# The second 16-bit part of queries and keys subtracted on GpSimd instead of VectorE

## The reference, cut to what matters

```
q, k, v = (heads(wq, bq), heads(wk, bk), heads(wv, bv))
q = _apply_rope(q, cos, sin)
k = _apply_rope(k, cos, sin)
att = jnp.einsum('bhtd,bhsd->bhts', q, k) * scale
...                                   # causal mask, softmax, times v
x = _layernorm(x + attention)
x = _layernorm(x + experts)           # gate, up, silu, down; weighted sum of 8 rows
```

## Time and profile before

| | |
|---|---|
| median of 3 runs | 2205.56 us (2202.02 to 2207.1) |
| profiled execution | 2201.4 us, span of its instructions 2199.6 us |
| mean granted TensorE clock | 0.935 of full speed |
| PE, DVE, ACT, POOL busy | 1818.1, 1600.4, 1357.2, 1245.4 us |
| L1653, the subtraction, on DVE | 32 instructions |
| L884, the row scatters, on POOL | 512 instructions, 530.4 us busy |

### The profile page before, as it was taken

The page is one execution under the profiler, slowest core; times in us unless marked ns, Lnnn a source line. Parts: engine busy times, 40 slices in busy tenths (PEclk is TensorE's granted clock), DMA queues, the critical chain, the costliest instruction groups (busy, mean ns, idle before and its releaser), DMA issues. The chain is left out here.

```text
span 2199.6 us, 53918 instructions
## 1 busy us (share of the span) xinstructions
PE 1818.1 (83%) x17104; PEld 1298.8 (59%) x17104; DVE 1600.4 (73%) x3572; ACT 1357.2 (62%) x3265; POOL 1245.4 (57%) x1206
## 2 busy tenths in 40 slices
PE   4899888988898889888987997989888888989930
PEld 2455554554555445454544886878777777878720
DVE  3788777877889788777873554565447778869988
ACT  1566655665655455554544876788776777888830
POOL 1003455446444654556544777777777777777760
PEclk8999999999999999999988999999999999999975
DMA  5466677667756875667666865656688899989977
GB/s 165 135 186 195 210 249 232 191 218 245 235 189 219 288 239 191 209 230 240 199 197 240 282 198 189 214 172 207 213 289 294 295 305 313 301 274 354 368 240 252
DMA packets 290570, 520.19 MB, mean 236 GB/s; under 512 B 46328, under 2 KB 192191, under 8 KB 280528
## 3 DMA queue, kind: packets, MB, share of 16 engines
q1 hardware_dynamic: 206400, 324.46, 47.1%
q0 software_dynamic: 58368, 163.70, 20.1%
q10 hardware_dynamic: 25536, 28.58, 3.9%
HBM read 284.54 MB, written 259.20 MB: 247 GB/s over the span
## 5 line engine op out<-in xcount | busy, mean ns | idle before, releaser
L1297 ACT ACTIVATE pT<-ps 128x512 f32<-128x512 f32 (+2 forms) x1008 | 676.6, 703 | 394.4 <-PE ps L1073 312.2
L884 POOL DMA_INDIRECT x_sorted<-xhl,idx x512 | 530.4, 1036 | 500.5 <-DVE xhl L1735 229.0
L1660 DVE TENSOR_REDUCE mn<-ps 128x1 f32<-128x512 f32 (+3 forms) x704 | 412.6, 632 | 57.5 <-PE ps L1047 55.1
L1139 PE MATMUL ps<-pT,gu_hi 128*128 128x256 f16 (+1 forms) x1600 | 372.1, 251 | 42.3 <-ACT pT L1297 42.1
L1140 PE MATMUL ps<-pT,gu_hi 128*128 128x256 f16 (+1 forms) x1600 | 371.1, 250 | 0.0
L1141 PE MATMUL ps<-pT,gu_lo 128*128 128x256 f16 (+1 forms) x1600 | 371.0, 250 | 0.0
L902 POOL DMA_INDIRECT y_tokens<-work,yidx x264 | 279.2, 1058 | 79.8 <-issue 61.8
L1045 PE MATMUL ps<-stacks 96*128 96x512 bf16 (+3 forms) x1024 | 274.7, 311 | 45.0 <-DVE mn L1660 24.0
L1071 PE MATMUL ps<-stacks 99*128 99x512 bf16 (+3 forms) x1024 | 285.7, 310 | 16.2 <-ACT pT L1297 12.6
L1073 PE MATMUL ps<-maskk,identb 128*128 128x128 bf16 x1024 | 223.0, 223 | 0.0
L1205 PE MATMUL ps<-dn,vx 128*128 x608 | 168.0, 276 | 49.3 <-DVE cosT L1868 14.6
(11 more groups left out here) (255 smaller groups left out, 3866.7 us busy)
## 6 DMA issues: line engine op xcount, KB each, us to landing
stacks<-y_tokens SPq DMA_DIRECT2D x64, 1024.0 KB
stacks<-qk_parts SPq DMA_DIRECT2D x128, 384.0 KB
qk_parts<-pbuf SPq DMA_DIRECT2D x62, 384.0 KB
attention<-yev ACTq DMA_DIRECT2D x64, 256.0 KB
qk_parts<-pbuf SPq DMA_DIRECT2D x62, 256.0 KB
stacks<-x_sorted SPq DMA_DIRECT2D x52, 304.0 KB, 4.4
x_sorted<-pads_h SPq DMA_DIRECT2D x99, 152.0 KB
pbuf<-x_sorted SPq DMA_DIRECT2D x40, 304.0 KB
```

The costliest lines, as they stand in the source:

```text
L884: pool.indirect_dma_start(xsort[g][:, :], bass.IndirectOffsetOnAxis(ap=at, axis=0), xhl_rows[:, t, :], None).then_inc(s_scat, 16)
L1139: mmul(o, w_hi[k], x_hi[k], start=k == 0, stop=False)
L1297: return nc.scalar.activation(o, i, f, **k)
L1660: V.tensor_reduce(mn[:, tt, h0:h0 + nh], ps[:, odd_bank("max", at, m), 0:nh * n].rearrange("p (a n) -> p a n", a=nh), axis=AX.X, op=ALU.ma ...
```

## The change

The subtraction of the parts leaves DVE's list inside the loop and enters POOL's, in front of the scatters of steps 5 and 11. Operands, waits and the semaphore that it raises stay the same. Batch 0's two subtractions ahead of the loop stay on DVE, so 30 of the 32 move.

```diff
@@ POOL @@
+            def last_part(b, n):
+
+                at = 2 * b + n
+                wait(pool, s_rest, at + 1)
+                wait(pool, s_part, part_count(b, n, 1))
+                nc.gpsimd.tensor_tensor(parts(b, n)[:, :, 2, :], rotated(b, n)[:, :, :], parts(b, n)[:, :, 1, :],
+                                ALU.subtract).then_inc(s_pp, 1)
...
             for i in range(NB):
                 for e in range(STEPS):
+                    if i < NB - 1:
+                        for n in range(2):
+                            if e == SLOT_LAST[n]:
+                                last_part(i + 1, n)
                     routing(i, e)
@@ DVE @@
                             if e == SLOT_REST[n]:
                                 rest(i + 1, n)
-                            if e == SLOT_LAST[n]:
-                                last_part(i + 1, n)
```

## The result

The changed kernel takes 2223.93 us (median of 7 runs, 2217.94 to 2231.88), the kernel before beside it 2207.1 us (7 runs, 2202.02 to 2216.66). The ratio is 1.0082 (95% interval 1.0057 to 1.0107): 0.8% slower, 17 us by the medians. The profiled execution took 22.4 us longer in span, 2222.0 against 2199.6 us.

What follows compares the result with a forecast made beforehand. It took a train of transfers in a full queue, releasing DVE and PE, as the bound: 14 x 1.28 = 17.9 us on 2201.4 gives 2219.3, or 2223.5 over the median; forecast 2221, 8-in-10 range 2206 to 2238.

Steps and rivals of the forecast that it cites:

- What bounds the turn: In each batch's pass, queued transfers from the queries' parts to the reciprocals' landing hold DVE's multiplication and PE; 21.1 us.
- The rival by which the shift is absorbed: Landing depends on the reciprocals' issue, not the first transfer's start; about 2205 us, no change; chance 0.15.
- POOL's duration: Each moved subtraction takes 2.5 us on POOL, range 0.90 to 2.95, so the queries' one ends 1.28 us late.
- The scatters behind it: POOL's later scatters fall behind, but their end costs nothing; about one more among the queued transfers, 0.4 us, left to range.
- The sign that I had named for this: From the queries' subtraction's end to DVE's multiplication should stay near 21 us in turn 4.
- The sum: Turns 1 to 14 lose 1.28 us each, 17.9 us; turn 0 and the expert stage nothing.
- POOL as the bound: Subtraction takes 2.95 us and late scatters add 0.4 us in 13 turns; 2231 us; chance 0.17.
- The rotation: DVE's `rotate` starts 0.40 us late, beside the transfers' 1.28; DVE idles 0.5 to 1.5 us before `rope` of the keys.
- The keys: POOL's keys' subtraction delays SP's issue of their parts by 1 us, covered because SP has nothing behind them until 384.93.
- The wait for the landing: DVE's wait for `xTden` grows from 48.6 us by more than 1.28 a turn, since DVE also arrives earlier.
- The clock: PE's clock falls to 0.50 as PE resumes; a longer stand-still may keep it low longer, a possible error.
- VectorE as the bound: Freeing DVE of subtractions ahead of row maxima pays if POOL takes under 1.22 us; about 2192 us; chance 0.08.

Runs made afterwards that it cites:

- The late train alone: Kernel before with one more wait on SyncE, so the queries' parts are issued later, after VectorE's first rope step of the keys; 2216.1 us, 1.0063.
- queries only: Changed kernel with the keys' subtraction back on VectorE, only the queries' one on GpSimd; 2233.1 us, 1.0131 to the kernel before.
- keys only: Changed kernel with the queries' subtraction back on VectorE, only the keys' one on GpSimd; 2201.55 us, 0.9985 to the kernel before.
- subtracted twice: Kernel before with the queries' subtraction in the loop done twice on VectorE, the second raising the semaphore; 2217.11 us, 1.0067.
- scatters late only: Kernel before with GpSimd doing an unread stand-in subtraction at the same two places, real subtractions staying on VectorE; 2214.23 us, 1.005.
- the same, root early: Kernel before with GpSimd's unread stand-in subtractions and its reciprocal root moved from behind step 19's scatters to behind step 17's; 2198.23 us, 0.9976.
- train and scatters late, root early: Kernel before with SyncE's extra wait before the queries' parts, GpSimd's unread stand-in subtractions and the earlier reciprocal root; 2221.61 us, 1.0086.

## Why the prediction was right, step by step

The time was forecast at 2221 us and came out at 2223.93; the place and the way of the loss were right, and two sizes were off in opposite senses.

*What bounds the turn.* Right. The late train alone gives 1.0063, and in the changed kernel the landing moved while the reciprocals' issue kept its place. The rival by which the shift is absorbed falls in turns 2 to 14. Turn 1, which has no scatters, stays open: there the landing, from ACT's copy, was 18.05 us before and 17.80 after, but 19.08 with the train late alone. Two readings of the DMA engines were too wide. They were not lightly used all the way up to 358: the share 0.31 is of the last 3 us, and from 349 to 352 it was 0.81. Nor is the queue full throughout: from the issue of the parts to the multiplication the share is 0.93 on the mean over turns 2 to 14, and 0.90 in the changed kernel.

*POOL's duration.* The mis-sized term. I took 2.5 us as the middle of two ways to stack memset passes; it is 2.13. The subtraction is 0.90 us longer, not 1.28, and the sum by this term is 14 x 0.90 = 12.6 us in place of 17.9. The figure of the Trainium skill ("GPSIMD Engine Reference", "Performance versus the Vector engine") would have come nearer: half of its 4497 ns, as an estimate, is 2.25 us, and the trace agrees to 0.12.

*The scatters behind it.* I let their end cost nothing and left their part in the train to the range. Their end did cost nothing in the changed kernel, where the wait for the root is 3.7 us as before. But the landing moved by 1.49 us a turn, 0.59 more than POOL's extra 0.90, and that is the term I left out: over 13 turns 7.7 us. The sign that I had named for this, about 21 us from the end of the queries' subtraction to the multiplication in turn 4, hid it: it reads 21.25 there, but over turns 2 to 14 the mean went from 19.67 to 20.21.

The count of scatters seems to contradict this: 11.3 in the train before, 11.0 in the changed kernel. What it hides is the first us behind the issue. The parts' own packets start only 0.8 us after their issue. In the kernel before 0.85 of a scatter starts in that first us, and the DMA engines' share in it is 0.50. In the five kernels of the table that hold the scatters at the queries' place none does, and the share is 0.10 to 0.12. So 0.4 us of the engines stand empty, and I take that scatter to ride in the train instead. By the last column, the landing should move by the train's delay and 0.41 us for each scatter more than 10.46:

| kernel | worked out, us | measured, us |
|---|---|---|
| the change | 0.95 + 0.22 = 1.17 | 1.49 |
| queries only | 1.93 | 2.27 |
| keys only | -0.62 | -0.46 |
| train late only | 1.11 | 1.14 |
| subtracted twice | 0.71 | 0.73 |
| scatters late only | -0.22 | -0.08 |
| the same, root early | -0.24 | -0.16 |
| train and scatters late, root early | 1.27 | 1.40 |

So the scatters let go inside the train (0.22 us) and POOL's start 0.05 us later behind the copy make about half of the 0.59 that the sum lacked. What is left, at most 0.34 us, is hardly above the 0.3 on which I don't build, and it stays open. The count ends at the landing and so depends on it; it is an account of these runs and no test of its own.

*The sum.* As turn 1 did not move, 13 x 0.90 = 11.7 us and 7.7 make 19.4, beside 20.4 measured in the attention stage and 17 in the medians. The agreement of 17.9 with these is in part luck: a subtraction taken 0.38 us too long stood in for a train taken 0.59 us too short.

*POOL as the bound.* That rival had the term which the sum lacked, 0.4 us in 13 turns for late scatters in the train. Its long subtraction did not come, and the reciprocal root was not late.

*The rotation.* I had it 0.40 us late, beside the train. The numerators' issue came 0.07 us later after the subtraction's start (mean 8.28 against 8.21 us). DVE waited 25.2 us for POOL in 14 turns, 1.8 us each, above my 0.5 to 1.5: the reduction in front of it was done even sooner than I took.

*The keys.* In turn 4 their parts go out 17.94 us after the queries' subtraction starts in place of 16.94, 1 us late and covered, as forecast; alone they are 0.9985. I had not seen that the hole which they make in the scatters helps the train.

*The wait for the landing.* I expected it to grow by more than 1.28 us a turn, since DVE would arrive earlier. It grew from 48.6 to 57.0 us, 0.6 a turn, since DVE arrived later (last section).

*The clock.* The sign that it stays low longer did come: from the copy to the multiplication the mean granted clock fell from 0.95 to 0.92. Behind the multiplication, where PE resumes, it is 0.95 in both kernels, and that stretch did not get longer (670.6 and 669.0 us).

*VectorE as the bound.* Falls: 30 x 1.223 = 36.7 us of subtraction left DVE's list, and the attention stage became longer.

## What to carry to other kernels

Before an operation is moved off a busy engine, look for who waits for its result: here a 0.9 us slower subtraction stood at the head of a train of transfers, and the engine that was relieved was waiting for that train's end. What an engine issues late counts as much as what it computes late: GpSimd's scatters share the DMA engines with the train and its list with a reciprocal root. And a second DMA queue need not free a load from the train in the first one: here it brought the landing 0.85 us of 21 forward, and a late train still made it 1.40 us late.

## What the runs showed that I had not expected

DVE's maximum for the weights' preparation (256 numbers from two tiles in SBUF) never took more than 428 ns in the kernel before. In the changed one it took up to 3106 where it met the keys' subtraction. The group by its line, minimum, median and maximum in ns, before and after:

```profile
L1594 DVE TENSOR_TENSOR prep<-prep x32: 411/418/428, 93.9 to 650.9; 128x256 f32<-128x256 f32 x32
```

```profile
L1606 DVE TENSOR_TENSOR prep<-prep x32: 411/418/3106, 89.0 to 655.8; 128x256 f32<-128x256 f32 x32
```

In turn 4 it runs from 371.02 to 373.48, POOL's subtraction from 371.03 to 373.18. In the next turn the two rows on DVE and POOL are:

```profile
446.65 3.10 DVE L1606 TENSOR_TENSOR prep<-prep 128x256 f32<-128x256 f32 x1
```

```profile
447.32 2.13 POOL L919 TENSOR_TENSOR pbuf<-qf,pbuf 128x1024 bf16<-128x1024 f32 x1
```

With queries only on POOL all 32 of them take 418 ns on the mean, and with keys only 639, so it is the keys' subtraction beside them that does it. The Trainium skill, "SBUF — State Buffer", section "Who interferes with whom", says that a VectorE instruction with two inputs in SBUF and a GpSimd instruction that reads SBUF exclude each other, and that the order of issue decides which of them waits. The trace agrees that one waits for the other, and in the run with the late scatters it agrees on the order: VectorE's subtraction opens 0.04 us first and keeps its 1.22 us, and the stand-in takes 3.05 us in place of 2.01. In the rows above the order can't be read: DVE's opens 0.67 us before POOL's and closes 0.30 us behind it, though with its 0.42 us alone it would have ended before POOL's row opens. Here the wait for the landing covered it, 13.8 us of busy time in all (27.2 against 13.4); on the turn's path it could have cost as much.
